# Attention and a gated expert layer on one core: GpSimd rounds a head's shift, two engine programs are written out, and the expert weights are loaded and split before attention ends

## The reference

```python
xn = _layernorm(x, axis=-1)
x = x + _L0_attn_ref(xn, ...) + _L0_ffn_ref(xn, ...)

# attention: 16 heads of 16 features
q = (xn @ Wq.T + bq) * SCALE;  k = xn @ Wk.T + bk;  v = xn @ Wv.T + bv
probs = softmax(einsum('bhqd,bhkd->bhqk', q, k));  out = (probs @ v) @ Wo.T + bo

# experts: each of 16 experts takes the 1024 tokens with the highest route value of a batch
h = gelu(einsum('ebld,edf->eblf', xg, w1) + b1)
out = einsum('eblf,efd->ebld', h, w2) + b2        # added back at the token's place
z = xn + outs;  return layernorm(z) * gamma + beta
```

## Time and profile before

| | |
|---|---|
| Median of 3 runs | 3384.15 us (3382.39 to 3384.70) |
| Profiled execution: time, span | 3384.77 us, 3383.0 us |
| Granted TensorE clock, mean of the span | 0.989 |
| PE, DVE, ACT, POOL busy | 3289.2 (97%), 2901.3 (86%), 2524.3 (75%), 933.5 (28%) us |
| Attention, from the first score to the last product with v | 257.5 to 2915.6 us |
| Expert stage | 2917.1 to 3383.0 us |

### The profile page before, as it was taken

How to read it: one execution, slowest core, us unless ns; L and a number is a source line. 1 busy time by engine, 2 the same in 40 slices (tenths; PEclk the granted TensorE clock), 3 DMA queues, 4 the chain that set the end, 5 groups by cost and what they waited for, 6 DMA issues and landing times. The chain is left out here.

```text
span 3383.0 us, 75004 instructions
## 1 busy us (share of the span) xinstructions
PE 3289.2 (97%) x20848; PEld 1702.7 (50%) x20848; DVE 2901.3 (86%) x2989; ACT 2524.3 (75%) x5724; POOL 933.5 (28%) x1340
## 2 busy tenths in 40 slices
PE   7999999999999999999999999999999999799998
PEld 6444444444444444444444444444444444488887
DVE  7758899999999999999999999999999998377777
ACT  3557788888888888888888888888888888544333
POOL 2550222222222222222222222222222222244443
PEclk9999999999999999999999999999999999899999
DMA  5783333333333333333333333333333332455554
GB/s 197 200 236 47 54 55 54 55 54 55 55 59 58 57 57 59 59 55 59 55 55 54 54 54 55 54 54 55 54 55 57 58 58 42 117 158 158 166 158 118
DMA packets 140694, 271.93 MB, mean 80 GB/s; under 512 B 30192, under 2 KB 76336, under 8 KB 128112
## 3 DMA queue, kind: packets, MB, share of 16 engines
q1 hardware_dynamic: 138144, 266.71, 37.4%
q10 hardware_dynamic: 2256, 1.36, 0.2%
HBM read 173.59 MB, written 84.93 MB: 76 GB/s over the span
## 5 line engine op out<-in xcount | busy, mean ns | idle before, releaser
L921 DVE TENSOR_REDUCE half_max<-m_ps 128x1 f32<-128x1024 f32 x2006 | 2363.5, 1220 | 223.9 <-PE m_ps L848 212.0
L802 ACT ACTIVATE prob<-s_ps 128x512 f32<-128x512 f32 (+1 forms) x5120 | 2191.1, 521 | 425.6 <-PE s_ps L858 417.0
L858 PE MATMUL s_ps<-q_feat,k_feat 50*128 50x512 f32 (+1 forms) x5120 | 1542.9, 397 | 13.8 <-ACTq L792 5.9
L848 PE MATMUL m_ps<-k_feat,q_feat 48*128 48x512 f32 x4012 | 1358.8, 444 | 20.3 <-DVE half_max L921 20.2
L858 PEld LDWEIGHTS s_ps<-q_feat,k_feat 50*128 50x128 f32 x5120 | 798.8, 185 | 994.7 <-ACT prob L802 880.9
L867 PE MATMUL a_ps<-prob,v_head 128*32 128x512 f32 x8192 | 1096.2, 607 | 0.0
L848 PEld LDWEIGHTS m_ps<-k_feat,q_feat 48*128 48x128 f32 x4012 | 599.0, 186 | 221.7 <-DVE half_max L921 211.3
L657 POOL TENSOR_TENSOR shift<-row_max,shift 128x16 fp32r<-128x16 f32 x63 | 14.0, 222 | 1164.1 <-ACT shift L809 1164.1
L867 PEld LDWEIGHTS a_ps<-prob,v_head 128*32 128x32 f32 x8192 | 161.4, 108 | 256.3 <-issue 217.8
L1221 ACT ACTIVATE g_hi<-g 128x512 fp32r<-128x512 f32 x128 | 81.0, 632 | 251.0 <-DVE g L1263 210.8
L1385 POOL TENSOR_TENSOR g_lo<-g,g_hi 128x512 fp32r<-128x512 f32 x128 | 173.5, 1355 | 224.3 <-ACT g_hi L1221 224.2
(11 more groups left out here) (147 smaller groups left out, 2000.5 us busy)
## 6 DMA issues: line engine op xcount, KB each, us to landing
q_feat<-q_parts SPq DMA_DIRECT2D x384, 128.0 KB, 4.2
k_feat<-k_parts SPq DMA_DIRECT2D x384, 128.0 KB, 5.6
q_parts<-parts SPq DMA_DIRECT2D x32, 512.0 KB, 4.3
k_parts<-parts SPq DMA_DIRECT2D x32, 512.0 KB, 4.4
att_dram<-att SPq DMA_DIRECT2D x64, 256.0 KB, 6.3
mask_bc<-mask_b SPq DMA_DIRECT2D x128, 128.0 KB, 4.5
x_in<-in_x SPq DMA_DIRECT2D x16, 512.0 KB, 4.2
xn_dram<-xn SPq DMA_DIRECT2D x16, 512.0 KB, 4.8
```

Source lines behind the costliest of these rows:

```text
L802: act.activation(prob[tile(r, kt) % R][:, cols(j)], s_ps[slot(r, kt, j) % R][:, wide(j)], ACT.Exp).then_inc(exped, 1)
L848: ins = pe.matmul(m_ps[p % 2][:, k * BLK:(k + 1) * BLK], q_feat[r % 2][LOW, qt * P:(qt + 1) * P], k_feat[r % 2][LOW, key:key + BLK], start ...
L858: pe.matmul(s_ps[slot(r, kt, j) % R][:, wide(j)], k_feat[r % 2][UP, kt * P:(kt + 1) * P], q_feat[r % 2][UP, cols(j)], start=True, stop=Tru ...
L921: dve.tensor_reduce(half_max[r][:, p // 2, p % 2:p % 2 + 1], m_ps[p % 2][:, :], AX.X, ALU.max).then_inc(maxed, 1)
```

## The change

Three things change.

1. In attention, `round_shift` goes from ACT to POOL: `split_shift` waits for `row_max` itself, rounds it with a copy, and takes the remainder as before.
2. The attention programs of ACT and DVE are written out, head after head, in place of loops of ten rounds. The loops of PE, POOL and SP stay.
3. The weights w1 and w2 and the bias b1 are loaded while attention is still under way, into memory that v no longer needs (the first three batches of `v_all`), and DVE makes both parts of w1 and w2 there, behind the inverses. The first block's token halves and first masks are loaded there too. In the expert stage the six pieces are gone; the sums of the second half and the halves of block 1 are issued before `b2_rows`, and DVE inverts the sums in four parts between the gates of the first block.

```diff
+SUMS_AT = 4 * S
+INV_AT = SUMS_AT + BLK
+LATE_AT = INV_AT + PARTS * BLK // 2
+LATE_LEFT = (B - 1) * H * ST * HD - (LATE_AT + KC * E * F + BLK + EP)
...
+        with nc.sbuf_tensor("v_all", [P, B, H, ST, HD], F32) as v_all:
+            pass
...
     CUTS = (0, BLK, 2 * BLK, 3 * BLK, 3 * BLK + BLK // 2, S)
@@ -619,9 +640,12 @@
     masked, mask_stored, mask_chain = sem("a_masked"), sem("a_mask_stored"), sem("a_mask_chain")
     spare = t["v_all"][:, :, :, :, :].rearrange("p b h s d -> p (b h s d)")
     gt, eq, cum = (spare[0:B * E, k * S:(k + 1) * S] for k in range(3))
+    w1_hi, w1_lo, w2_hi, w2_lo = (t[w][:, :, :].rearrange("p c n -> p (c n)") for w in ("w1_hi", "w1_lo", "w2_hi", "w2_lo"))
+    raw = spare[:, LATE_AT:LATE_AT + KC * E * F], spare[:, S:2 * S]
+    raw_in, raw_rounded, weights_split = t["raw_in"], t["raw_rounded"], t["weights_split"]
     mask16 = spare[0:B * E, 3 * S:3 * S + S // 2].bitcast(BF16)
-    sums = spare[:, 4 * S:4 * S + BLK]
-    inv_parts = spare[:, 4 * S + BLK:4 * S + BLK + PARTS * BLK // 2].bitcast(BF16).rearrange("p (k s) -> p k s", k=PARTS)
+    sums = spare[:, SUMS_AT:INV_AT]
+    inv_parts = spare[:, INV_AT:LATE_AT].bitcast(BF16).rearrange("p (k s) -> p k s", k=PARTS)
...
             def split_shift(n, r):
-                pool.wait_ge(shift_rounded, n + 1)
+                wait_apart(pool, shift_turned, n, t["passed"][2])
+                wait_apart(pool, row_maxed, n + 1, t["passed"][2])
+                pool.tensor_copy(shift[:, 0, :], row_max[r][:, :]).then_inc(shift_rounded, 1)
+                wait_apart(pool, shift_rounded, n + 1, t["passed"][2])
                 pool.tensor_tensor(shift[:, 1, :], row_max[r][:, :], shift[:, 0, :].bitcast(F32), ALU.subtract).then_inc(shift_done, 1)
...
             sp.wait_ge(att_out, 16 * (P // BPS + 1))
             sp.dma_start(sums, sum_rows(t, 0)).then_inc(sums_in, 16)
+            sp.dma_start(raw[0].rearrange("p (c n) -> p c n", c=KC), t["w1"].rearrange("(c p) n -> p c n", p=P)).then_inc(raw_in[0], 16)
+            sp.dma_start(t["b1_col"][:, :], t["b1"]).then_inc(t["b1_in"], 16)
...
             sp.wait_ge(prepared_out, 32 * HALVES + 16)
             sp.wait_ge(masked, 1)
             sp.dma_start(t["mask_b"], mask16).then_inc(mask_stored, 16)
+            sp.dma_start(raw[1].rearrange("p (c n) -> p c n", c=EP), t["w2"].rearrange("(c p) n -> p c n", p=P)).then_inc(raw_in[1], 16)
+            sp.wait_ge(mask_stored, 16)
+            sp.dma_start(t["xn_hi0"][:, :].bitcast(F32).rearrange("p (n s) -> p n s", n=KC),
+                         t["tok_hi_dram"][0:KC].rearrange("n p s -> p n s")).then_inc(t["xn_in"][0], 16)
+            sp.dma_start(t["xn_lo0"][:, :].bitcast(F32), t["tok_all"][:, 0, :]).then_inc(t["xn_in"][0], 16)
+            first_masks = t["mask_bc0"][:, :, :]
+            for k in range(2):
+                src = t["mask_b"].rearrange("(b e k) s -> b k e s", b=B, k=2)[0, k, 0:EP // 4, 0:BLK]
+                sp.dma_start(first_masks[k * F:(k + 1) * F, :, :],
+                             src.unsqueeze(0).broadcast_to([F, EP // 4, BLK])).then_inc(t["masks_in"][0], 16)
             sp.wait_ge(inverted, 1)
             sp.dma_start(t["inverse_dram"][0:P], inv_parts).then_inc(inverse_stored, 16)
-            sp.wait_ge(mask_stored, 16)
             sp.wait_ge(inverse_stored, 16)
             sp.wait_ge(att_out, 16 * HEADS)
             put_att(HEADS - 1)
...
-            def round_shift(n, r):
-                if not (isinstance(n, int) and n == 0):
-                    act.wait_ge(shift_turned, n)
-                act.wait_ge(row_maxed, n + 1)
-                act.activation(shift[:, 0, :], row_max[r % R][:, :], ACT.Copy).then_inc(shift_rounded, 1)
...
-            step(0, 0, first=True)
-            step(1, 1)
-            with nc.Fori(0, ROUNDS, engines=[ENGINE.Activation], hint_back_edge=True, head_slot={ENGINE.Activation: 40}) as i:
-                for r in range(2, U + 2):
-                    step(i * U + r, r)
-            for g in range(2 + ROUNDS * U, HEADS):
-                step(g, g, following=g + 1 < HEADS)
+            for g in range(HEADS):
+                step(g, g, first=g == 0, following=g + 1 < HEADS)
...
-            maxima(2, 2)
-            with nc.Fori(0, ROUNDS, engines=[ENGINE.DVE], hint_back_edge=True, head_slot={ENGINE.DVE: 16}) as i:
-                for k in range(U):
-                    maxima(i * U + R + k, k % R)
-            maxima(HEADS - 1, (HEADS - 1) % R)
+            for n in range(2, HEADS):
+                maxima(n, n % R)
...
+            dve.wait_ge(masked, 1)
+            for k, (hi, lo) in enumerate(((w1_hi, w1_lo), (w2_hi, w2_lo))):
+                dve.wait_ge(raw_in[k], 16)
+                dve.tensor_copy(hi, raw[k]).then_inc(raw_rounded, 1)
+                dve.wait_ge(raw_rounded, k + 1)
+                dve.tensor_tensor(lo, raw[k], hi.bitcast(F32), ALU.subtract).then_inc(weights_split, 1)
...
+            sp.wait_ge(t["att_out"], 16 * (HEADS + 1))
+            sp.dma_start(sums[:, :], sum_rows(t, 1)).then_inc(sums_in, 16)
             masks(0, 1)
             quotients(0)
+            halves(1, 1)
             tokens(0)
             sp.wait_ge(b2_split, 1)
             for k in range(PARTS):
                 sp.dma_start(b2_rows[k * E:(k + 1) * E, :], b2_parts[:, k, :]).then_inc(b2_placed, 16)
-            sp.wait_ge(t["att_out"], 16 * (HEADS + 1))
-            sp.dma_start(sums[:, :], sum_rows(t, 1)).then_inc(sums_in, 16)
-            halves(1, 1)
...
-                pe.wait_ge(piece_split, 1 + W1_AT[e // 2])
...
-                pe.wait_ge(piece_split, 1 + W2_AT[e // 4])
...
-            for dst, src in ((b2_sb[:, :], t["b2"]), (b1_col[:, :], t["b1"]), (gamma_bc[:, :], t["gamma"].partition_broadcast(P))):
+            for dst, src in ((b2_sb[:, :], t["b2"]), (gamma_bc[:, :], t["gamma"].partition_broadcast(P))):
...
-                    if first and AHEAD_PIECES + e < len(pieces):
-                        round_piece(AHEAD_PIECES + e)
...
-            for k in range(AHEAD_PIECES):
-                round_piece(k)
             act.activation(t["warm"][:, :], t["ident"][:, 0:1], ACT.Gelu)
-            act.wait_ge(small_in, 16 * 3)
+            act.wait_ge(t["b1_in"], 16)
...
+            def invert_sums(k):
                 dve.wait_ge(sums_in, 16)
-                do(dve.reciprocal(sums[:, :], sums[:, :]))
...
+                dve.reciprocal(part, part).then_inc(inv_chain, 1)
+
...
                     gate(blk, e)
-                    if not last and AHEAD_PIECES + e < len(pieces):
-                        split_piece(AHEAD_PIECES + e)
-                    if not last and e == 4:
-                        invert_sums()
-                    if not last and e == 5:
-                        split_inverses()
+                    if not last and 1 <= e <= 2:
+                        invert_sums(2 * e - 2)
+                        invert_sums(2 * e - 1)
+                    if not last and 3 <= e < 2 + PARTS:
+                        split_inverses(e - 3)
+                    if not last and e == 2 + PARTS:
+                        last_inverses()
```

92 lines of the change are left out of this document (33 added, 59 removed).

## The result

The changed kernel took 3340.11 us (median of 4 runs, 3336.90 to 3341.13), the one before 3384.10 us beside it: a ratio of 0.9869 [0.9852, 0.9886], 44 us less. The forecast was 3346, with a range from 3336 to 3361. The profiled execution of the changed kernel took 3341.13 us for a span of 3339.4 us.

What follows compares the result with a forecast made beforehand. PE was taken to set attention's pace, the passage to the expert stage as second bound. Attention 22.6 plus passage 15.5 made 38.1; 3384.77 less 38.1 and 0.6 gave 3346 us, range 3336 to 3361.

Steps and rivals of the forecast that it cites:

- The entries, edges and exit: Attention loops of ACT and DVE: entries 13.6 us, ACT's exit 3.9, DVE's back edges 4.2, ACT's 0.9; 22.6 won.
- The exit's 3.9 us: Last long attention head, after ACT's loop: 45.07 us against an ordinary 41.13, so 3.9 us won by writing out.
- an ordinary head takes 41.13 us: Attention: time between starts of `row_max`, 41.13 us, from which the longer heads' savings were counted.
- The rounding: Attention: moving the shift's rounding from ACT to POOL wins 0 us; 6.05 us hide POOL's copy and remainder.
- Loads and splits ahead of the boundary: End of attention: DVE's four weight operations, at most 13.0 us, covered by 16 us of PE's last head; counted 0.
- The passage: Attention into the expert stage's block 0: first gelu 11.7 us earlier, block end 2948.8 instead of 2964.32; 15.5 us won.
- the masks are queued behind `b2_rows` on SP: Block 0, gate of pair 4: its mask wait stays, since `b2_rows` waits for POOL's `b2_split`; gate at 2937.3.
- keep their pace: Expert-stage blocks after block 0: no change in their time.
- Straight code runs dry: Rival, attention: written-out ACT and DVE stall on instruction fetch, 87 us lost less 38 won, 3433 us; chance 0.05.
- The stalls at the entries are those of new code: Rival, loop entries: fresh code stalls anyway, so only back edges, exit and passage win, 24.5 us, 3360; chance 0.09.
- The rounding comes late: Rival, attention: POOL comes late and each head waits a microsecond, 63 us more, 3409; chance 0.01.
- The passage keeps its length: Rival, passage: masks of pair 2 or 4, or TensorE's clock, eat most of the gain; 27.6 us won, 3356; chance 0.08.

Runs made afterwards that it cites:

- x1: Kernel before with only DVE's attention program written out, rounding still on ACT: 3366.76 us against 3380.71, ratio 0.9962.
- x2: Kernel before with only ACT's attention program written out, rounding still on ACT: 3371.73 us against 3380.71, ratio 0.9971.
- x4: Changed kernel with both loops and ACT's rounding put back, leaving early loads, splits and first block's new order: 3366.26 us against 3380.71 before, ratio 0.9963.
- x6: Kernel before with DVE's loop made one round of sixty heads, folded in the build to a branch: 3365.96 us against 3380.79, ratio 0.9954.
- x3: Kernel before with only the rounding moved from ACT to POOL, both loops kept: 3378.33 us against 3380.71, ratio 0.9997.
- x8: Changed kernel with the rounding put back on ACT: 3340.77 us against 3380.79 for the kernel before, ratio 0.9880.
- x7: Changed kernel with the `b2_split` wait and `b2_rows` loads moved behind the masks of pairs 4 to 7: 3340.12 us against 3384.72 before, ratio 0.9871.
- x10: Changed kernel with first-block masks issued ahead of quotient operands, tokens and `b2_rows`: 3335.05 us against 3380.79 before, ratio 0.9864.
- x5: Kernel before with both ACT's and DVE's attention programs written out, nothing else: 3355.15 us against 3380.79, ratio 0.9926.
- x9: Changed kernel with waits for the split weights put back into PE's every `hide` and `unhide`: 3340.28 us against 3384.72 before, ratio 0.9870.

## Why the prediction was right

**The number.** 38.1 us were forecast and 44.0 measured. Nearly all of the difference is the 5.8 us missed in attention. The 2.3 us that the first stretch gained and the 2.3 that the last one lost stood in no forecast, and it is luck that they cancel.

**The entries, edges and exit (22.6).** The mechanism holds, engine by engine: x1 and x2 each remove their own engine's gaps and no others, and after the change every place is an ordinary head. The three numbers read from the heads' lengths, 13.6, 3.9 and 4.2, are all found again. The 13.6 do not divide cleanly: DVE alone gives 7.2 of them and ACT alone 4.2, since either stall, left alone, still takes PE to its lower clock. Windows of x1 and then of x2 behind their one gap at the entry (the seventh column is the granted clock) show it:

```profile
345.00:355.00 10.00, 8.73 (x39) 3.74 (x40) 4.81 (x4) 6.75 (x15) 3.53 (x5) 0.66 0.78 151
```

```profile
335.00:345.00 10.00, 10.00 (x42) 4.03 (x46) 6.35 (x7) 5.65 (x13) 2.11 (x3) 0.50 0.01 3
```

Of x2's head, 9.35 us over an ordinary one, the stall is 3.10; the rest goes with the lower clock behind it. The changed kernel has 1.00 between 345 and 355.

The exit's 3.9 us are a size read from one execution, and that it came out was partly luck. ACT has the same kind of gap in the head after its loop in every kernel that keeps the loop (1.90 us before, 1.62 in x1, x4 and x6, 1.18 in x3), but the head costs 0.8 to 1.2 us more than an ordinary one in x3, x1 and x4, 2.5 in x6 and 3.9 before. The granted clock tells them apart. Windows of the kernel before, then of x4:

```profile
2840.00:2845.00 5.00, 3.94 (x23) 1.52 (x21) 3.18 (x3) 3.21 (x7) 0.00 (x0) 0.88 0.01 2
2845.00:2850.00 5.00, 5.00 (x24) 2.55 (x23) 2.38 (x3) 3.00 (x7) 0.00 (x0) 0.50 0.00 0
...
2830.00:2850.00 20.00, 19.21 (x128) 8.96 (x124) 17.05 (x16) 15.89 (x38) 0.00 (x0) 1.00 0.04 12
```

Before, PE was at its lower clock behind the gap; in x4, as in x1 and x3, it kept the full one, and x6 lies between (0.78 over five microseconds). From x4's lengths, the same forecast would have been 12.2 for the entries and 1.2 for the exit.

**What was missed in attention (5.8 of 28.4).** The step that failed is the one that read an ordinary head as fixed: "an ordinary head takes 41.13 us", and every saving was counted from there. The loop's body had a cost in every head, 0.09 us behind `row_max`, 5.6 us in 62 heads. There were two signs of it. PE waited for DVE 58 times between 420 and 2800, 16.4 us in all, in the same view as the earlier trace rows, above the lines taken. And the one head that lies before both loops took 329.56 - 288.57 = 40.99 us, not 41.13. "A faster ACT or DVE brings nothing by itself" was wrong there.

**The rounding (0).** Right as far as x3 and x8 can tell: 0.19 us for the copy, 0.95 us from the start of `row_max` to the end of the remainder in POOL, against a turn that comes 6.16 us behind it.

**Loads and splits ahead of the boundary (0).** Right, and safer than bounded: 7.0 us of DVE instead of at most 13.0, done at 2867.25, 19.2 us ahead of the boundary. DVE waited 5.42 us for w2, and PE did not feel it: from the last `row_max` to the boundary it is 55.6 us before and after.

**The passage (15.5; 15.3 in the profile after, 16.6 in x4).** The total holds, its steps less so. The first gelu came 3.70 us behind the boundary, not 2.75, and so missed the sign that was set for it (under 3.5): ACT's table load starts 1.55 behind it instead of 1.35, and 0.66 us of issue stand ahead of the gelu. The gate of pair 4 came at 20.05 and was forecast at 20.25; the wait stayed, as said. The cause given, "the masks are queued behind `b2_rows` on SP", is only half of it. It set the time of issue (15.1 us behind the boundary), but x7 issued the masks 6.6 us earlier and they landed no sooner, behind the bulk. So the bulk by itself holds them too, and with both out of the way (x10) the wait went. What `b2_rows` alone would cost, without the bulk, no run shows; an estimate from the rows, issue at 15.1 and 3.4 us to land, puts the gate at 18.5 or later.

**Later blocks "keep their pace".** They lost 0.08 us each. The starts of `num_hi` in blocks 2 and 10 of the changed kernel, then in x5, blocks 2 and 10:

```profile
2972.09 1.04 ACT L1225 ACTIVATE num_hi<-num 128x1024 fp32r<-128x1024 f32 x1
...
3186.75 1.04 ACT L1225 ACTIVATE num_hi<-num 128x1024 fp32r<-128x1024 f32 x1
```

```profile
2987.53 1.05 ACT L1231 ACTIVATE num_hi<-num 128x1024 fp32r<-128x1024 f32 x1
...
3201.56 1.05 ACT L1231 ACTIVATE num_hi<-num 128x1024 fp32r<-128x1024 f32 x1
```

214.66 / 8 = 26.83 and 214.03 / 8 = 26.75. All kernels with the passage's code have the first and all without it the second, so it comes with that code. From the first `num_hi` to the last it makes 1.0 of the 2.3 us that the end lost (402.5 against 401.5). The other 1.3 lie behind the last `num_hi`, a piece that took 17.2 to 18.6 us in kernels with and without that code, so they are not put down to the change. PE's waits are not the cause of the 0.08 (x9). The new places of weights and operands in memory are what I would try next; that was not tried, and the cause is open.

**The rivals.** *Straight code runs dry* did not happen: ACT and DVE fetch all of attention as straight code, and neither shows an issue wait between 420 and 2800. The Trainium skill ("Runtime: NRT & Kernel Launch", Instruction fetch mechanics) says that sequential prefetch mostly hides this and a taken branch outside the window does not; both rows agree, the absent line after and the 4.1 and 1.8 us of the nine edges before. Whether the edges' targets lay outside that window no run shows. *The stalls at the entries are those of new code* is refuted by x1 and x2, where the same heads are new code too and the gap goes with the loop. *The rounding comes late* is refuted by the 4.68 us that POOL stands idle before it. *The passage keeps its length* did not happen, and what held pair 4 cost 3.2 to 5.7 us (x10), not the 10.5 that this rival needed.

## What to carry to other kernels

A loop of an engine that is not the bottleneck can hold the bottleneck in two ways, and they are read in two places: the stalls at its entry, back edges and end as longer periods of the slowest engine, and the work of its body as a short wait that comes once per period. Sum such waits by line before a period is called ordinary, and take the sum as a bound: of the 0.21 us that PE stood in an ordinary head, 0.09 were won here. A stall's price read from one execution holds the clock of that execution; look whether the granted clock fell behind it before the price is counted as sure.

Where an instruction waits for a small transfer, look at what was issued just ahead of it and not only at what its queue waited for. Two things held the masks here, and taking one away moved nothing. In the stretch whose DMA share was near one, small loads issued behind bulk landed late, and moving the bulk that is needed late, with `b2_rows`, behind the small transfers that are needed soon was worth 3.2 to 5.7 us here.

## What the runs showed of the hardware

- Entering a loop stopped DVE for 3.1 us and ACT for 4.4 to 5.0 us (waits of issue at that place: 3.06 and 4.80 before, 3.07 and 4.91 in x3, 3.05 and 5.04 in x4, 4.38 and 4.89 on ACT in x1 and x6, and 3.10 on DVE in x2), and a branch without a loop 0.1 us or less (x6). The Trainium skill ("Advanced Engine Details and Errata", Control Flow Timing) gives 51 and 108 ns for branches; x6 agrees with that, and the entries and the 0.45 us of DVE's back edge do not come from the branch alone.
- Such a stall costs PE more than its length: 4.38 us on ACT alone made the head 6.4 us longer, and PE ran at a lower granted clock behind it (0.66 of full over ten microseconds, 0.50 in x2).
- The end of ACT's loop cost 0.8 to 3.9 us (last head 41.90 in x3, 42.21 in x1, 42.33 in x4, 43.59 in x6, 45.07 before). The gap is 1.2 to 1.9 us; the heads of 43.59 and 45.07 are those where the granted clock fell behind it, to 0.78 and 0.50 of full over five microseconds. Before it fell to 0.50, PE had been busy 3.94 of 5.00 us. What decides whether it falls is open.
- A 128 KB load of masks took 3.4 to 4.2 us from issue to landing in the changed kernel, where it was issued at 2901.61 and after, and 6.0 to 11.5 in x7, issued behind the bulk while the DMA share was 1.05.
- Behind a 0.19 us reduction on DVE the next one starts 0.10 us after its start in straight code and 0.19 in a loop's body with register instructions. Behind a transposition of 0.20 us it starts 0.28 after in both.
